# Where a step's four maximum tiles stand among its score matmuls (first attention)

## What is computed

```python
qkv = x @ W_qkv + b_qkv
q, k, v = (qkv[:, :, 0], qkv[:, :, 1], qkv[:, :, 2])
k = k + pos_enc[None, :, None, :]
scores = jnp.einsum('bqhd,bkhd->bhqk', q, k) / scale
attn = jax.nn.softmax(scores, axis=-1)
out = jnp.einsum('bhqk,bkhd->bqhd', attn, v)
...
return out @ W_out + b_out
```

## Time and profile before

| | us |
|---|---|
| median of three runs (lowest, highest) | 2144.91 (2139.06, 2145.79) |
| the profiled execution | 2144.52 |
| its span in the trace | 2142.7 |

### The profile page before, as it was taken

The page is one execution under the profiler, slowest core; times in us unless marked ns, Lnnn a source line. Parts: engine busy times, 40 slices in busy tenths (PEclk is TensorE's granted clock), DMA queues, the critical chain, the costliest instruction groups (busy, mean ns, idle before and its releaser), DMA issues.

```text
span 2142.7 us, 35861 instructions
## 1 busy us (share of the span) xinstructions
PE 2060.6 (96%) x12074; PEld 945.5 (44%) x12074; DVE 1692.1 (79%) x2739; ACT 1702.3 (79%) x2299; POOL 1284.4 (60%) x777
## 2 busy tenths in 40 slices
PE   6999999999999999999999989999999999999996
PEld 2544445445444445454454433333333433443445
DVE  7677787877877878777887837789999999999903
ACT  1678888888888888888888984388878878888883
POOL 1588898897997987988988795333032024016003
PEclk7899999999999999999999998599999999999998
DMA  3000000000000000000000100000000000000000
GB/s 105 20 16 20 27 16 31 16 17 30 16 28 19 16 31 16 27 20 16 31 16 27 40 16 20 1 1 2 2 1 1 2 2 7 1 2 6 1 2 11
DMA packets 32039, 36.33 MB, mean 17 GB/s; under 512 B 12340, under 2 KB 23228, under 8 KB 31736
## 3 DMA queue, kind: packets, MB, share of 16 engines
q1 hardware_dynamic: 31864, 34.03, 5.1%
HBM read 32.46 MB, written 1.43 MB: 16 GB/s over the span
## 4 chain that ended last, share of the span: by engine, by line
PE 80%; ACT 7%; DVE 6%; issue 3%; POOL 3%; DMA 0%; DVEq 0%; ACTq 0%; POOLq 0%
PE acc_o L538 18%; PE scores L516 14%; PE acc_o L658 11%; PE scores L644 10%; PE ring L491 8%; ACT prob L846 3%; DVE mxp L1521 3%; PE ring L624 2%; POOL accp L1016 2%; PE ring L708 2%; PE ring L717 2%; ACT prob L868 2%; PE ring L468 2%; ACT scores L853 2%; PE ring L456 2%
## 5 line engine op out<-in xcount | busy, mean ns | idle before, releaser
L1404 DVE TENSOR_REDUCE mxp<-ring 128x1 f32<-128x512 f32 x1024 | 656.3, 685 | 231.3 <-PE ring L491 214.6
L1016 POOL TENSOR_TENSOR accp<-accp,prob 128x1024 f32<-128x1024 f32 x318 | 799.8, 2515 | 54.5 <-ACT prob L846 11.0
L868 ACT ACTIVATE prob<-scores 128x512 f32<-128x512 f32 x1024 | 545.3, 601 | 135.6 <-PE scores L644 132.9
L846 ACT ACTIVATE prob<-scores 128x1024 f32<-128x1024 f32 x512 | 520.0, 1016 | 147.1 <-PE scores L516 127.9
L516 PE MATMUL scores<-q_all,k_all 64*128 64x512 f32 x3072 | 545.4, 409 | 7.2 <-ACT scores L853 4.9
L1521 DVE TENSOR_REDUCE mxp<-ring 128x1 f32<-128x512 f32 x789 | 510.7, 684 | 52.4 <-PE ring L624 39.9
L853 ACT ACTIVATE scores<-minus_all 128x1024 f32<-128x1024 f32 x510 | 525.2, 1030 | 24.2 <-ACT prob L846 0.8
L538 PE MATMUL acc_o<-prob,v 128*64 128x512 f32 x2048 | 500.3, 609 | 2.9 <-ACT v L828 2.9
L491 PE MATMUL ring<-k_all,q_all 64*128 64x512 f32 x1024 | 392.8, 432 | 10.1 <-DVE mxp L1404 5.5
L516 PEld LDWEIGHTS scores<-q_all,k_all 64*128 64x128 f32 x3072 | 336.2, 186 | 84.8 <-ACT scores L853 41.2
L644 PE MATMUL scores<-q_all,k_all 32*128 32x512 f32 x1024 | 308.1, 494 | 12.7 <-ACT prob L868 8.5
(11 more groups left out here) (197 smaller groups left out, 1553.9 us busy)
## 6 DMA issues: line engine op xcount, KB each, us to landing
minus_all<-m_dram SPq DMA_DIRECT2D x32, 512.0 KB, 3.6
rec<-rec_dram SPq DMA_DIRECT2D x60, 128.0 KB, 2.8
w_all<-w_pairs SPq DMA_DIRECT2D x1, 1344.0 KB, 11.2
x<-x SPq DMA_DIRECT2D x4, 256.0 KB, 3.8
pos_sb<-pos SPq DMA_DIRECT2D x1, 1024.0 KB, 7.6
w_all<-w SPq DMA_DIRECT2D x1, 1024.0 KB, 5.6
minus_all<-w SPq DMA_DIRECT2D x4, 256.0 KB, 3.6
q_all<-m_rows SPq DMA_DIRECT2D x64, 2.0 KB
```

What stands on the lines that cost most here:

```text
L846: nc.scalar.activation(prob[:, T % SLOTS1, :, :], sc[T % 2][:, :, :], ACT.Exp, scale=SCALE1).then_inc(exp_done, 1)
L868: nc.scalar.activation(prob2[:, h // 2, T % 2, h % 2, :], sc2[place % 3], ACT.Exp, scale=SCALE2).then_inc(exp2_done, 1)
L1016: nc.gpsimd.tensor_tensor(accp[:, k % 2], accp[:, k % 2], prob[:, T % SLOTS1], ALU.add).then_inc(pool_acc, 1)
L1404: done(nc.vector.reduce_max(mxp1[k % 2][:, h * QT + q, kc:kc + 1], bank[:], AX.X), ("max", k, q, kc, h))
```

## The change

`sides1` gives the first two of a step's four tiles to the place ahead of the first score set, the other two to the place between the sets, and none to the place behind the second. It was one, two and one. The order of the tiles among themselves, and so the banks they use, stays.

```diff
@@ -130,7 +130,7 @@
         if cp:
             tiles += [("max", *cp, h) for h in range(2)]
         tiles += tiles_late1(k, j, half)
-    return tiles[:1], tiles[1:3], tiles[3:]
+    return tiles[:2], tiles[2:], []
```

## The result

The changed kernel takes 2208.6 us (median, 2203.6 to 2211.2) against 2143.5 us for the kernel before: a ratio of 1.0296, 95% interval 1.0278 to 1.0313. The forecast was 2201 us, slower, with a range of 2165 to 2222. The profiled execution took 2206.8 us, 62.3 us more than that of before; the sum forecast 56.4.

What follows compares the result with a forecast made beforehand. TensorE, busy for 96% of the span, was taken to set the end, with some steps waiting for ScalarE. Terms 59.1 + 0.7 - 3.4 = +56.4 us on 2144.5 gave 2201 us, range 2165 to 2222.

Steps and rivals of the forecast that it cites:

- The bank wait of m3: Each step's fourth maximum tile waits for the first one's bank: starts at 1.35, item or values at 2.48 us.
- m1's move costs nothing: Second maximum tile, moved ahead of the first score set: that set's last matmul still starts at 0.80, no matmul time lost.
- ScalarE's old wait is swallowed, the two don't add: Steps 2, 4 and 7: seed ends at 1.14 of the next step, before 1.35, so the new wait covers the old.
- The lag of VectorE in chunks with k projections (+0.34 in step 1): A late add delays step 1's first reduction; the fourth tile waits 0.34 us longer, +2.14 for such a chunk.
- Chunks with v projections have no lag: Other chunks: a step 0 longer by 0.43 us takes away the add's lag into step 1; +1.80 us per chunk.
- rival 4: VectorE's adds run late in two more steps of each chunk: 20 us more, 2221; beyond 2222: 3%.
- 26 x 1.97: 1.97 us is the forecast mean loss per chunk, from +2.14 with a key projection and +1.80 without.
- 59.8 forecast: Forecast loss ahead of the last chunk: +59.1 us for chunks 0 to 29 and +0.7 for chunk 30.
- The last chunk: Tiles of 32 rows, visited twice instead of three times a step: eight steps save up to 0.43 each, -3.4 us.
- Rival 1: Same-half neighbours on TensorE cost 0.23 us a step; alternation gives back 56 us: 2145 (4%) or 2089 (3%).
- Rival 2: ScalarE's seed sets the second score set's start in nearly every step anyway: -56 us, 2089 us; chance 3%.
- Rival 3: The bank wait is smaller, without 0.13 us from release to matmul: 32 us less, 2169; chance of 2150 to 2178: 7%.

Runs made afterwards that it cites:

- the short reductions: VectorE's maximum reductions read only 256 of 512 columns: 2135.5 us in the order of the kernel before, 2138.5 us in the changed order.
- third experiment: Kernel before, no tile moved, but each couple's half 1 tile ahead of its half 0 tile, so halves alternate: 2142.1 us, ratio 0.9986.
- ninth experiment: Kernel before, with the changed order only in step 7 of chunks with v projections and in the last chunk: 2141.9 us, ratio 0.9988.
- sixth experiment: Changed kernel, but in step 1 of a chunk VectorE's add goes ahead of the reduction of the fourth maximum tile: 2199.0 us, ratio 1.0241.
- seventh: Kernel before, with the changed order only in step 7 of each chunk and in the last chunk: 2173.2 us, ratio 1.0142.
- fourth: Kernel before, in its own order, but VectorE's maximum reductions read only 256 of 512 columns: 2135.5 us, ratio 0.9961.

## Why the prediction was right, point by point

- *The bank wait of m3.* Right in place and size: m3 at 1.37 (forecast 1.35), values at 2.46 (2.48), item-free step 4.33 (4.35). Shown by the run that moved m3 alone, which lost all of it, and by the short reductions, which took it away.
- *m1's move costs nothing.* Right; the run with m1 alone kept the steps of before from chunk 2 on.
- *ScalarE's old wait is swallowed, the two don't add.* Right: in step 7 of chunk 10 the second set starts 1.37 after m0 with m3, not at 1.54, and the item at 2.46, as forecast 0.2 us sooner than before.
- *The lag of VectorE in chunks with k projections (+0.34 in step 1).* Wrong. I let VectorE's add shift with the item. In chunk 12 it started 0.42 us later after the m0 of step 0 (4.37, not 3.95), but was held up by GpSimd's add in both kernels, which ended at 4.82 and 4.84, and itself ended at 5.90 and 5.92: the longer step took the lag away. The forecast also took steps 2 and 7 from chunk 10, though in chunks with k projections they took 5.39 and 5.70 us before, not 5.24 and 5.61; they went to 5.19 and 5.41. These chunks lost 1.6 us, not 2.14.
- *Chunks with v projections have no lag.* Wrong by more: their step 2 lost 1.33 us instead of gaining 0.04, since an order of two adds tipped over 0.13 us. They lost 3.05 us, not 1.80. This is the term that was mis-sized, and it is not the one that rival 4 had spread (0.34 in two steps of every chunk): it is four times as large and sits in one step of half of the chunks. Both errors together: chunks 2 to 27 lost 60.5 us, against 26 x 1.97 = 51.2 forecast. That is the 9 us by which the 68.5 at the last chunk exceed the 59.8 forecast. (Projections of k and v stand only in chunks 0 to 27, 14 chunks of each kind; the forecast counted 15. Chunks 28 and 29, without them, lost 1.9 and 1.6.)
- *The last chunk.* Forecast -3.4, measured -2.1: in a plain step it went from three visits of tiles to two, 4.93 to 4.53 us from values to values. Steps 2 to 5 gained 0.40 to 0.44 each (1.7 in all), as taken; steps 0 and 1 together and step 6 gained nothing, which the "eight steps" of the forecast had counted in. Why is not shown.
- *Rival 1*, the rule on row groups: 3 us of 56 (third experiment). The sentence of the Trainium skill that the prediction cites stands in Part 3 of its page, under "The mechanism". The trace speaks against it: m0 and the first score matmul both use half 0, and the weight load of the latter starts at 490.93, 0.01 us after m0, when m0 is running. *Rival 2*: true only of steps that already wait for a seed, and there only with the bank free in time (ninth experiment). *Rival 3*: the release cost was 0.11 us to the weight load and 0.14 to the matmul, as taken.

That 2201 stands 8 us from the measured 2208.6 owes something to luck: the error in the chunks with k projections took back part of the one in the chunks with v projections, and the stretch behind the first attention was 4 us shorter.

## What to carry to other kernels

Where buffers go round in a ring of n, an operation can't move ahead of the release of the one n before it, however little its own engine has to do there; count uses and compare with the end of the reader before moving it, and move it only where the in-order engine would stand still anyway. Then look at what each shift of a tenth of a microsecond does to operations of VectorE and GpSimd that start close together: which of them comes first can be worth more than the shift. It costs only where work that another engine waits for stands behind the delayed add.

## What the runs showed of the hardware

- An add of 128x1024 on VectorE takes 1.21 us ahead of one on GpSimd and 3.40 us when it starts 0.05 to 0.06 us behind it; GpSimd's own takes 2.37 to 2.38 us when first and 3.38 to 3.39 us when second. When VectorE's was second, it ended 1.07 to 1.09 us after GpSimd's in each pair shown. Such a difference of starts moved the last chunk by 17.6 us (sixth experiment) and a whole kernel by some 30 us (seventh), which was not expected; in the fourth it cost nothing.
- Two 64-row matmuls of the same half next to each other, m0 and the first score matmul, start 0.01 us apart, and making all neighbours alternate changed a step by at most 0.05 us. The start times alone can't say how the array does this.
- A reduction of a PSUM bank takes 0.69 us for 512 columns and 0.42 us for 256.
